# Weights of the second message pass of layer 1 built on VectorE, its one-hot tables on ScalarE, and one bias add on GpSimd

## The reference, cut to what matters

```python
z2 = h1 @ W2.T
e2 = _leaky((z2 @ a2[:OUT_DIM])[src] + (z2 @ a2[OUT_DIM:])[dst])
alpha2 = _segment_softmax(e2, dst, n)
out = jax.ops.segment_sum(alpha2[:, None] * z2[src], dst, num_segments=n)
...
attn = v + t2                       # mix of layer 1
return attn @ W_out + b_out
```

## Time and profile before

| | |
|---|---|
| median of the runs | 5609.07 us |
| the profiled execution, its own time | 5609.07 us |
| its span (first to last instruction) | 5606.7 us |
| L2: first gather to the end of the last | 3585.96 to 4769.11 us |
| from there to the first instruction behind the meeting | to 4798.77 us |

### The profile page before, as it was taken

The page is one execution under the profiler, slowest core; times in us unless marked ns, Lnnn a source line. Parts: engine busy times, 40 slices in busy tenths (PEclk is TensorE's granted clock), DMA queues, the critical chain, the costliest instruction groups (busy, mean ns, idle before and its releaser), DMA issues.

```text
span 5606.7 us, 76465 instructions
## 1 busy us (share of the span) xinstructions
PE 4071.5 (73%) x18105; PEld 2851.1 (51%) x18105; DVE 3341.8 (60%) x10049; ACT 3181.1 (57%) x7675; POOL 3307.6 (59%) x3443
## 2 busy tenths in 40 slices
PE   3997666666662596577777776577877785797998
PEld 3564554445442594355555544456665664333565
DVE  5377766666667666577777776655565564522111
ACT  2365666666661232477777776478788886443222
POOL 0124777777764755677777776577777777012222
PEclk9998877887785597798898898799899988898999
DMA  4293554544541344454444443344444444200110
GB/s 128 70 281 102 142 140 141 140 140 138 140 127 50 109 139 128 140 135 136 135 134 135 134 134 109 117 129 129 132 132 131 132 132 128 87 23 27 35 34 27
DMA packets 349467, 658.92 MB, mean 118 GB/s; under 512 B 80930, under 2 KB 198704, under 8 KB 348760
## 3 DMA queue, kind: packets, MB, share of 16 engines
q0 software_dynamic: 156336, 433.90, 28.3%
q1 hardware_dynamic: 182928, 211.64, 12.8%
q10 hardware_dynamic: 9772, 8.50, 0.5%
HBM read 539.67 MB, written 115.45 MB: 117 GB/s over the span
## 4 chain that ended last, share of the span: by engine, by line
PE 22%; POOL 16%; issue 15%; DMA 7%; DVE 5%; ACT 4%; DVEq 0%; POOLq 0%; SPq 0%; ACTq 0%
POOL AR L1000 11%; DMA AR<-D_z,SRCI 6%; PE ps L1236 5%; PE ps L2686 4%; PE ps L2667 4%; PE ps L2374 3%; ACT AR L1291 2%; POOL AR L1702 2%; PE ps L2386 1%; POOL D_sx L1692 1%; PE ps L2154 1%; ACT AR L1283 1%; POOL AR L1830 1%; PE ps L1196 1%; PE ps L2290 1%
## 5 line engine op out<-in xcount | busy, mean ns | idle before, releaser
L1000 POOL DMA_INDIRECT AR<-D_z,SRCI x1856 | 1794.0, 967 | 634.3 <-issue 500.3
L1236 PE MATMUL ps<-AR 128*128 128x264 f32 (+2 forms) x5568 | 1692.3, 456 | 233.2 <-DVE AR L1097 138.5
L1236 PEld LDWEIGHTS ps<-AR 128*128 128x128 f32 x5568 | 1214.4, 227 | 543.0 <-issue 271.4
L1000 POOL DMA_INDIRECT AR<-D_h,SRCI x904 | 873.9, 967 | 277.4 <-issue 239.0
L1283 ACT ACTIVATE AR<-iota_n,NREL 128x128 f32<-128x128 f32 x2784 | 881.1, 389 | 34.8 <-PE ps L1236 30.5
L1119 DVE TENSOR_TENSOR AR<-ps,AR 128x264 f32 (+2 forms) x1392 | 589.3, 423 | 212.6 <-DVE AR L1119 131.3
L1097 DVE TENSOR_TENSOR AR<-AR,ps 128x1024 f32<-128x1024 f32 x464 | 558.3, 1203 | 0.1
L1033 DVE TENSOR_TENSOR AR<-AR 128x128 f32<-128x128 f32 (+2 forms) x174 | 49.0, 282 | 784.2 <-SPq L981 784.1
L1291 ACT ACTIVATE AR<-AR 128x128 f32<-128x128 f32 x928 | 382.1, 482 | 7.7
L1204 PE MATMUL ps<-ident,AR 128*128 128x128 f32 (+2 forms) x174 | 56.8, 326 | 422.2 <-DVE AR L1035 422.2
L1308 ACT ACTIVATE AR<-ps 128x128 f32<-128x128 f32 (+2 forms) x174 | 47.1, 271 | 534.8 <-PE ps L1204 529.6
(11 more groups left out here) (447 smaller groups left out, 7794.5 us busy)
## 6 DMA issues: line engine op xcount, KB each, us to landing
AR<-D_rel SPq DMA_DIRECT2D x348, 256.0 KB
D_sx<-AR SPq DMA_DIRECT2D x8, 6370.0 KB
AR<-D_z,SRCI POOLq DMA_INDIRECT x1856
AR<-D_h,SRCI POOLq DMA_INDIRECT x928
D_y<-AR SPq DMA_DIRECT2D x106, 128.0 KB, 1.7
AR<-in_L_ffn_Wd SPq DMA_DIRECT2D x8, 1024.0 KB, 11.9
AR<-D_mask SPq DMA_DIRECT2D x58, 128.0 KB
D_h<-AR SPq DMA_DIRECT2D x49, 132.0 KB, 1.7
```

Source lines behind the costliest of these rows:

```text
L1000: e.indirect_dma_start(out=GV[:, u % 48, :], out_offset=None, in_=D_row[L.i], in_offset=bass.IndirectOffsetOnAxis(ap=SRCI[:, u:u + 1], axi ...
L1236: t = e.matmul(banks[n % 3][:, 0:YW], Sr[:, u % 8, :], GV[:, u % 48, L.GW - YW:L.GW], start=(i == 0), stop=(i == 1))
```

## The change

In L2, `spread` goes from ScalarE. In its place VectorE makes each unit's `S` with one instruction, in `weigh`: `S = (minus_n == NREL[u]) * WT[u]`, where `minus_n` is the row 0, -1, ..., -127, made once. That is 16 `tensor_scalar` a round, 928 in all, with two scalars that are read from SBUF. VectorE's `one_hot` goes, and ScalarE makes the tables as it does in L0 and L1: |.| and Relu over 128x1024 bf16, twice a round. ScalarE's copy into `WN` goes. The bias add of a block (L2097) goes from VectorE to GpSimd: ahead of unit u = 16 (b + 6) GpSimd waits for `o_added` of block b and adds the bias to `X[:, b, :]`, 49 times.

```diff
-        WT, WN = [[ART[:, NB * 257 + 65 + 32 * j + 16 * i:NB * 257 + 81 + 32 * j + 16 * i] for i in range(2)] for j in range(2)]
+        minus_n = ART[:, NB * 257 + 1:NB * 257 + 129]
+        WT = [ART[:, NB * 257 + 129 + 16 * i:NB * 257 + 145 + 16 * i] for i in range(2)]
...
-        def stream_gpsimd(e, L, begun=0):
+        def stream_gpsimd(e, L, begun=0, tile_added=None):
...
+                if tile_added and u % 16 == 0 and 0 <= u // 16 - 6 < NB:
+                    b = u // 16 - 6
+                    e.wait_ge(tile_added, b + 1)
+                    e.tensor_tensor(X[:, b, :], X[:, b, :], bo[:, :], ALU.add)
                 if u >= 48 and u % 2 == 0:
...
                 if L.weighted:
+                    for u in range(16 * g + 4 * q, 16 * g + 4 * q + 4):
+                        t = e.tensor_scalar(Sr[:, u % 8, :], minus_n[:, :], NREL[:, u:u + 1], WT[K % 2][:, u % 16:u % 16 + 1], ALU.is_equal, ALU.mult)
+                    t.then_inc(s_ready, 1)
                     return
...
-                if k + 1 < NG2 and L.weighted:
-                    one_hot(k + 1, 0)
...
-                if L.weighted:
-                    p = (L.k0 + g) % 2
-                    if q == 0:
-                        e.wait_ge(r_ready, L.k0 + g + 1)
-                    for i in range(4):
-                        t = e.activation(w[:, i, :], w[:, i, :], ACT.Relu, bias=WT[p][:, 4 * q + i:4 * q + i + 1], scale=WN[p][:, 4 * q + i:4 * q + i + 1])
-                    t.then_inc(s_ready, 1)
-                    return
...
-                    e.activation(WN[K % 2][:, :], w[:, 0:P], ACT.Copy, scale=-1.0).then_inc(*ac.up())
...
-                if g >= 0:
+                if g >= 0 and not L.weighted:
                     spread(g, 1)
                 side.after_spread1(e, k)
-                if k + 1 < NG2 and not L.weighted:
+                if k + 1 < NG2:
                     one_hot(k + 1, 0)
...
                     e.tensor_tensor(X[:, b, :], X[:, b, :], BK_O[:, 0:256], ALU.add).then_inc(o_added, 1)
-                    e.wait_ge(o_added, b + 1)
-                    e.tensor_tensor(X[:, b, :], X[:, b, :], bo[:, :], ALU.add)
...
-            stream_gpsimd(e, L2)
+            stream_gpsimd(e, L2, 0, o_added)
```

More of the change, by code:

```diff
@@ L1035, in scores @@
                 e.scalar_tensor_tensor(out=AD[:, 0:P], in0=AD[:, 0:P], scalar=L.slope, in1=AD[:, 0:P], op0=ALU.mult, op1=ALU.max).then_inc(e_ready, 1)
[L1037 to L1043, removed]
             def runs(k):
@@ L1128, in stream_vector @@
             e.memset(BW[0:1, 17 * H:17 * H + 1], -BIG)
+            if L.weighted:
+                e.tensor_scalar(minus_n[:, :], iota_n[:, :], -1.0, None, ALU.mult)
             e.memset(Yv, 0.0).then_inc(y_clear, 1)
             e.wait_ge(y_clear, L.i + 1)
-            if L.weighted:
-                one_hot(0, 0)
-                one_hot(0, 1)
             at = None
@@ L1164, in stream_vector @@
                 side.before_reference(e, k)
-                if k + 1 < NG2 and L.weighted:
-                    one_hot(k + 1, 1)
                 if more:
@@ L1321, in weights @@
                 e.activation(RR[:, 0:H], w[:, 128:128 + H], ACT.Exp).then_inc(r_ready, 1)
-            if not L.weighted:
-                one_hot(0, 0)
-                one_hot(0, 1)
+            one_hot(0, 0)
+            one_hot(0, 1)
             for g in range(-1, NG2):
@@ L1346, in stream_scalar @@
                 side.after_weights(e, k)
-                if k < NG2:
+                if k < NG2 and not L.weighted:
                     spread(k, 0)
```

## The result

| | before | after |
|---|---|---|
| median of the runs | 5609.02 us | 5653.79 us |
| ratio | | 1.0083 [1.007, 1.0095] |
| span of the profiled execution | 5606.7 us | 5651.6 us |
| first gather of L2 to the end of the last | 1183.15 us | 1233.05 us |
| tail to the next stage | 29.66 us | 26.82 us |

The kernel is slower by 44.8 us. It was forecast at 5633 us (5615 to 5657): slower, as forecast, by 21 us more than the likeliest value, and inside the range.

What follows compares the result with a forecast made beforehand. GpSimd's uninterrupted list of gathers was taken to bound L2. Adds +33.3, collisions -11.2 and +2.5, tail -0.5 gave +24.1 us on 5609.07: 5633 us, with 5615 to 5657 for 8 in 10.

Steps and rivals of the forecast that it cites:

- The bound: L2: GpSimd never waits and sets the length; ScalarE's relief gives 0 us; VectorE waits for rows in every round.
- The adds: GpSimd in L2: 49 bias adds between gathers at 0.68 us each, +33.3 us (19 to 55).
- Rival 1: GpSimd in L2: the add hides the gather's 0.30 us gap, 0.39 us a place, +10 us, 5619 us; chance 0.12.
- The pace of the products: VectorE in L2: each new `S` instruction takes 0.26 us, 4.2 us a round (3.0 to 5.2).
- Collisions: L2 gathers lengthened by VectorE: 11.2 us go with L1043 and L2097, 2.5 us (1 to 6) return with 928 new instructions.
- the prediction's own sign: L2 gathers: a mean of 0.96 us was expected; a rise over 0.975 us would mean the collisions were misjudged.
- the forecast's own range: Whole kernel: 5620 to 5649 us, with the add at 0.5 to 0.95 us; the forecast's chance was 0.66.
- Rival 3: L2: each new VectorE instruction holds GpSimd for its whole length, 190 starts x 0.13 us; +46, 5655 us; chance 0.05.
- Rivals 2 and 4: Besides rival 2: in L2 ScalarE is what the round waits for, at PE's L2143; 5584 us; chance 0.04.
- rival 2: L2: VectorE or PE becomes the bound, cycle 21.3 to 21.6 us; about +45, up to 5663 us; chance 0.13.
- The tail: End of L2, last four quads: VectorE paces them at 2.3 us instead of ScalarE's 2.9; -0.5 us (-3 to +3).

Runs made afterwards that it cites:

- the kernel with the wait: Changed kernel plus a VectorE wait for its second scan before the four products; 1.008, 0.9951 and 1.0077 of the kernel before, on three chips.

## Why the prediction was right in its sign and 21 us short

**The bound: right.** GpSimd without a stop, VectorE waiting for rows, ScalarE's relief worth nothing. ScalarE was forecast at near 45% of L2 and is at 43%. VectorE's waits were forecast at 2 to 4 us a round and are 5.3. The round got 0.86 us longer instead of 0.4, which explains 0.5 of it; the rest I haven't traced.

**The adds: right.** +33.3 was forecast (19 to 55), 29.7 measured. The duration was 0.737 instead of 0.68; of the gap that I charged in full, 0.13 us is hidden. Rival 1, which hid all of it, would have given 21 us with this duration.

**The pace of the products: right.** 0.26 us was forecast. A group of four takes 1.08 us, and its instructions start 0.24 to 0.26 us apart.

**Collisions: the step that failed.** The forecast was -11.2 +2.5 = -8.7 us, and +20.3 came. By the prediction's own sign, a mean over 0.975 us, the collisions were misjudged: it is 0.992. The part that goes did go: outside the 53 held gathers, 41.1 - 30.5 = 10.6 us are left, against 20.5 - 11.2 + 2.5 = 11.8 by the forecast's own terms. What was missing are the 30.5 us at one place out of four. I had priced a product by the L431 of another stage, 0.026 us at each start, as if what counts were the instruction and how long it runs. The runs show that it is what stands right ahead of it. The same products cost a gather 0 to 0.15 us behind other instructions, and up to 0.81 us behind the two scans (1.07 in a later run). One of the others, L1083, is a TENSOR_TENSOR of 16x128 in SBUF with the products queued behind it and no wait between, and there the most is 0.14 us; so it takes more than an SBUF operation in front, and why it has to be these scans is open.

The term of the add came out 3.6 us lower and the tail 2.3 lower than forecast; the collisions were 29 us off, and the stages around L2 took 2.2 us less. The time lies outside the forecast's own range (5620 to 5649) and inside the range for 8 in 10, whose upper end of 5657 was there for rivals 2 and 3. That it lies inside is luck.

**Rival 3 gave nearly the right time (5655) by another mechanism.** It let every product hold GpSimd for its whole length at 190 starts. In fact 111 gathers start while a product runs, 53 gathers are held and the rest hardly at all, and a hold ends 0.78 us into a group of 1.08. The Trainium skill (SBUF — State Buffer, "Who interferes with whom") says of VectorE's two-port modes that whoever issues first has the shared pair for the whole instruction. For a product in three of the four groups the trace doesn't bear that out: it lasts 0.33 us, and the most that a gather loses there is 0.15. It also says that an instruction with at most one SBUF input, outside the two-port modes, doesn't contend: the run with the row in PSUM, where only the two scalars come from SBUF, agrees, with 1.8 us of stretch in place of 27.4 to 42.8.

**Rivals 2 and 4: refuted** by the waits for rows, in the profile at 5654 us. On the slower chips GpSimd does wait for PE, as rival 2 would have it, but the change as a whole costs nothing there (0.9984). GpSimd's hold on VectorE, which rival 2 counted at 0.4 us a round, is there as well: scans of 0.77 to 1.37 us instead of 0.41. In the profile at 5654 us it fell on no scan; all 114 take 0.45 us at most.

**The tail: right in sign.** -0.5 (-3 to +3) was forecast, -2.8 measured, near the low end. Which of its two terms was off I haven't traced.

Open: what the kernel would take at 5609 us without the held gathers. The hold is shown by taking it away in seven runs, but none of them was made where GpSimd is the bound. Open too: why the kernel with the wait takes 0.8% more than the kernel before on two chips and 0.5% less on a third. The wait alone isn't shown to be the reason: with the add on VectorE the same wait gives 1.0001 on one of the two. And it is open what makes PE stand still on these chips.

## What to carry to other kernels

If an engine works through its list without a stop, price a change by what is added to that list and by what makes its items longer; relief on the busiest engine by share was worth nothing here. For operations moved to VectorE beside a GpSimd that issues indirect DMAs, look at what stands directly ahead of each group: two scans with four SBUF products right behind them held GpSimd for up to 1 us, and a wait that delays VectorE by 0.11 us, or one operand in PSUM, took that away. Behind other instructions the same products held it for 0.15 us at most, so look for the long items in the trace and don't take every such row for a hold. And try a change on more than one chip, since the bound of the same stage was GpSimd at 5609 us and others at 6400.

## What the runs showed of the hardware

- Two scans and four `tensor_scalar` behind each other hold a gather in two pieces: one that starts during the first scan until the second scan ends, one that starts later, up to 0.43 us into the products, until 0.78 us behind their start. Some that start just as the second scan does slip through (six in the two runs with the add on VectorE), and then the products come 0.05 to 0.08 us late. The next gather starts 0.30 us after the held one as always, so nothing of it is caught up.
- With its column row in PSUM the product leaves GpSimd alone and takes 1.33 us for four instead of 1.08.
- An add of 128x256 f32 on GpSimd between two gathers takes 0.74 us and hides 0.13 of the 0.30 us gap; a scan on VectorE that overlaps it goes from 0.41 to 0.77 us or more (1.37 at most), and the add itself to 0.91 and, at most, 1.07.
- The same kernel takes 5609 us on one chip and 6375 to 6445 us on four others. Its instructions on VectorE, ScalarE and GpSimd last about the same (busy in L2 672, 897 and 886 us against 667, 905 and 900); the granted clock of TensorE in L2 is 0.80 instead of 0.88, PE is busy 85 us more, and the rest of the 285 us is time in which it stands still.
